# Attention scores in halves of 64 rows with 320 columns, masks as 64x64 triangles

## The chip, the cores and the metric

The kernel runs on one core of a Trainium2 chip. The metric is the device time of one execution in microseconds (us). The core has five engines that run beside each other and meet at semaphores: TensorE (PE, matmuls from SBUF into PSUM), VectorE (DVE), ScalarE (ACT), GpSimd (POOL) and SyncE (SP, which issues transfers). PSUM has 8 banks of 128 partitions with 512 f32 columns each.

## What is computed

A layer of attention and a mixture of experts on 4 x 1024 tokens of width 256, with 16 heads of width 16. What matters here is the attention, cut from the reference:

```python
xn = _layernorm(x, axis=-1)
q, k, v = heads(q), heads(k), heads(v)            # (4, 16, 1024, 16) each, from xn
attn = jnp.einsum('bhqd,bhkd->bhqk', q, k) / math.sqrt(DK)
mask = jnp.abs(idx[None, :] - idx[:, None]) > WINDOW      # WINDOW = 128
attn = jnp.where(mask[None, None], -1000000000.0, attn)
p = jax.nn.softmax(attn, axis=-1)
out = jnp.einsum('bhqk,bhkd->bhqd', p, v)
```

Each query sees the 128 keys on either side and itself. In tiles of 128 rows a tile of queries meets at most three tiles of keys: the previous one (a triangle of it), its own (whole), and the next one (a triangle).

## The kernel before

Projection, routing and experts come first (to about 740 us of the span), then the block `attend`, then `merge` (output projection, from about 1128 us). `attend` works through 64 pairs of batch and head in 16 groups of 4 heads (HG). A group has 8 rows j of 128 positions (TT). The scores are computed twice.

Query side, one group ahead: `scores_q` (matmul at L1459) has 128 queries on the partitions and up to 384 keys along the columns, in a ring of three banks (S1). DVE's `maxima` (L1626) adds the mask `mask_q` and takes each query's maximum, as a negative minimum, into `nmax`; each is an instruction on the tile and a short one that reads the accumulator. `split_maxima` splits them into a high and a low bf16 part, `turn_maxima` (PE, L1494) transposes them, `copy_maxima` (DVE, L1645) and four small transfers of SP put them as two more rows below the queries' parts, so that the second product subtracts the maximum by itself.

Key side, in the group itself: `scores_k` (L1467) has 128 keys on the partitions and up to 384 queries along the columns, in a ring of three banks (S2). `masks` (L1452) adds -1e30 outside of the window by a matmul of the identity with two stored 128x128 triangles, 256 columns in one instruction (interior rows) or 128 (rows 0 and 7, the edge rows). ACT's exponential (L1566) writes the tile `pT` to SBUF; `values` (L1480) multiplies it with the values, four heads in four column groups of 32 rows of one bank.

PE's order is written out: in row j, for each of four heads a key score with its mask and a query score of the group ahead; then the values of the row before; then in rows 0, 2, 3 and 5 a turn (of maxima at 0 and 5, of four output tiles, L1503, at 2 and 3), whose results go through the same ring of three S1 banks. DVE follows: the four maxima of a row, between them the additions of the gathered expert rows (L1664, L1680), the two normalisations (L1652, L1655), the splits and copies. A query score waits until DVE has freed the bank of three entries before (`s1_free`); a key score waits for the exponential of three heads before (`p_ready`). The first 32 query scores are taken among the last blocks of the experts (`score`, L1146, not touched). PE's loop over groups holds two of them, DVE's and ACT's one; first and last groups are written out. The last group has no query side.

Of the kernel before, what the change touches and what calls it, by code (L numbers as in the profile page):

```python
# [81 lines left out]
IOTA = 6 * P + 2 * MB  # L82
# [5 lines left out]
PARTS = (0, CUT), (CUT, TT)  # L88
PACK, PACK_BITS = 4, 6
# [19 lines left out]
def project(nc, ctx, x, w_qk, w_vr, w_exp, c_f32, keep):  # L109
# [158 lines left out]
    def vector(dve):  # L268
# [161 lines left out]
        nc.vector.tensor_copy(cb[:, :], consts[:, P:6 * P]).then_inc(consts_ready, 1)  # L430
# [170 lines left out]
def route(nc, ctx, keep, w_exp, left):  # L601
# [75 lines left out]
    def vector(dve):  # L677
# [57 lines left out]
        def table():  # L735
            for c in range(MB):
                chain.done(nc.vector.scalar_tensor_tensor(
                    junk[:, :], ends, consts[:, 6 * P + c:6 * P + c + 1], one, ALU.is_le, ALU.mult,
                    accum_out=cols[:, c:c + 1]))
                chain.wait()  # L740
# [194 lines left out]
def opening_tiles(nc, ctx):  # L935
# [3 lines left out]
    def sem(name):  # L939
# [3 lines left out]
        "mask_q": sb("mask_q", [P, 3 * P]), "masked": sb("masked", [P, 2, 3 * P]), "nmax": sb("nmax", [P, HG, TT]),  # L943
# [9 lines left out]
def experts(nc, ctx, keep, w_exp):  # L953
# [45 lines left out]
    ident_b, mask_prev, mask_next = (keep["cb"][:, k * P:(k + 1) * P] for k in (0, 3, 4))  # L999
# [31 lines left out]
    with nc.Block() as block:  # L1031
# [180 lines left out]
        def _(dve):  # L1212
# [61 lines left out]
            dve.wait_ge(o["mask_ready"], 3)  # L1274
# [7 lines left out]
def attend(nc, ctx, keep, onorm, w_proj):  # L1282
# [7 lines left out]
    ident_b, mask_prev, mask_next = (cb[:, k * P:(k + 1) * P] for k in (0, 3, 4))  # L1290
    both_masks = cb[:, 3 * P:5 * P]
# [7 lines left out]
    def sems(name, n):  # L1299
# [8 lines left out]
    mask_q, masked, nmax, nmax_b, nmaxT, nrow_in, s1_ready, s1_free, hi_done, nmax_ready, dve_tick, pe_tick = (  # L1308
        opening[name] for name in ("mask_q", "masked", "nmax", "nmax_b", "nmaxT", "nrow_in", "s1_ready", "s1_free",
# [9 lines left out]
    va_const, va_ready = sem("va_const"), sem("va_ready")  # L1319
# [64 lines left out]

    def key_back(j, hh):


        return {0: 2, 1: 2, 2: 5}.get(j * HG + hh, 3)
# [28 lines left out]
    with nc.Block() as block:  # L1417
# [25 lines left out]
        def _(pe):  # L1443

            def masks(bank, i, n):

                if i in (0, TT - 1):
                    out, mask = (bank[:, n - P:n], mask_next) if i == 0 else (bank[:, 0:P], mask_prev)
                else:
                    out = bank[:, 0:n].rearrange("p (t q) -> p t q", t=3)[:, 0:3:2, :]  # L1450
                    mask = both_masks.rearrange("p (t q) -> p t q", t=2)
                return nc.tensor.matmul(out, ident_b, mask, start=False, stop=True, skip_group_check=True)  # L1452

            def scores_q(g, q, i, hh):


                lo, hi = window(i)
                reach(pe, s1_free, ahead_entry(g, i, hh) - (RING - 1))
                nc.tensor.matmul(ring_bank(ahead_entry(like(g), i, hh))[:, 0:(hi - lo) * P], qk[0:KS, q, 0, hh, i * P:(i + 1) * P],  # L1459
# [484 lines left out]
```

## Time and profile before

| | |
|---|---|
| time, median of 3 runs | 1368.24 us (1366.77 to 1371.7) |
| span of the profiled execution, first to last instruction | 1166.2 us |
| time of the median outside of that span | 202.0 us |
| PE busy | 1085.4 us (93%), 8297 matmuls |
| PE weight loads busy | 799.0 us (69%) |
| DVE busy | 767.9 us (66%) |
| ACT busy | 756.1 us (65%) |
| POOL busy | 622.2 us (53%) |
| mean granted clock of TensorE | 0.984 |

Busy times are unions: two instructions beside each other count once. Matmuls are pipelined and their ends are modelled, so that the distance of two starts says more than a duration. The shares are over the whole span; the attention block is a third of it and has to be read by itself.

### The profile page before, as it was taken

To read this page: it belongs to the slowest core of one execution; us is meant where nothing else is said; L and a number is where in the kernel's file an instruction comes from. 1 tells how busy PE (TensorE), PEld (TensorE's weight loads), DVE (VectorE), ACT (ScalarE), POOL (GpSimd) and SP (SyncE) were. 2 spreads that over 40 slices of the span, in tenths; PEclk is the share of its full clock that TensorE was granted. 3 is DMA by queue.
4 is the path that set the end of the run, shared out by engine and by line. 5 is a ranking of instruction groups with operands and counts; after the bars stand their busy time and mean duration, and the time that the engine had idled before them with its cause. 6 is when DMAs were issued, how large, how long until landed. Compare 5 with 4: busy or idle time off the path is not lost. (4 is left out here: it accounts for less than half of the span.)

```text
span 1166.2 us, 33945 instructions
## 1 busy us (share of the span) xinstructions
PE 1085.4 (93%) x8297; PEld 799.0 (69%) x8298; DVE 767.9 (66%) x2491; ACT 756.1 (65%) x1914; POOL 622.2 (53%) x658
## 2 busy tenths in 40 slices
PE   6989799599999999999999999699999999999999
PEld 3545456399999999999999999355545545455457
DVE  7777779734444444444444457589999998999933
ACT  2555367567777777777777776366666666666653
POOL 0444200176666666666666655466666666666620
PEclk9999899899999999999999999799999999999999
DMA  6888811278888888878877764366665576656413
GB/s 223 216 213 213 240 42 32 94 222 261 247 251 244 252 253 240 250 240 250 253 229 205 206 198 149 101 154 159 154 171 142 142 169 161 152 143 159 122 60 122
DMA packets 143000, 213.84 MB, mean 183 GB/s; under 512 B 19425, under 2 KB 115682, under 8 KB 142946
## 3 DMA queue, kind: packets, MB, share of 16 engines
q0 software_dynamic: 27648, 86.02, 27.6%
q1 hardware_dynamic: 70946, 84.42, 25.9%
q10 hardware_dynamic: 44352, 42.74, 10.6%
q8 instruction: 26, 0.43, 0.2%
q14 instruction: 28, 0.23, 0.1%
HBM read 142.59 MB, written 70.26 MB: 183 GB/s over the span
## 5 line engine op out<-in xcount | busy, mean ns | idle before, releaser
L1076 POOL DMA_INDIRECT xb<-token_rows,idx_ring_x x320 | 303.1, 947 | 179.2 <-issue 140.5
L1104 PE MATMUL psum<-xTe,wb_and_xT_all_or_onorm 128*128 128x128 f32 x2560 | 339.2, 276 | 0.0
L1724 POOL DMA_INDIRECT yg<-expert_rows,idx_ring x256 | 254.2, 993 | 122.5 <-PE psum L1452 45.3
L1227 DVE TENSOR_SCALAR ys<-psum,xb 128x256 f32<-128x256 f32 x320 | 154.9, 484 | 244.7 <-PE psum L1113 243.3
L1104 PEld LDWEIGHTS psum<-xTe,wb_and_xT_all_or_onorm 128*128 128x128 f32 x2560 | 312.4, 192 | 0.1
L1566 ACT ACTIVATE pT<-psum 128x384 f32<-128x384 f32 (+1 forms) x512 | 215.5, 467 | 135.6 <-PE psum L1452 127.7
L1626 DVE CUSTOM_DVE_ANT_0 masked<-psum,mask_q 128x384 f32<-128x384 f32 (+1 forms) x480 | 230.9, 518 | 20.6 <-PE psum L1459 17.2
L1177 ACT COPY wb_and_xT_all_or_onorm<-wb_and_xT_all_or_onorm 128x512 f32 x320 | 197.7, 619 | 18.5 <-SPq L1038 4.8
L1113 PE MATMUL psum<-wb_and_xT_all_or_onorm,aT 128*128 x640 | 191.8, 381 | 0.4 <-issue 0.2
L1163 ACT COPY xTe<-psum 128x256 f32<-128x256 f32 x320 | 119.1, 372 | 102.4 <-PE psum L1094 93.0
L1459 PE MATMUL psum<-qk 96*128 96x384 bf16 (+1 forms) x480 | 154.0, 321 | 29.7 <-DVE nmax L1626 18.4
L1467 PE MATMUL psum<-qk 98*128 98x384 bf16 (+1 forms) x512 | 163.0, 320 | 4.0 <-POOL va L1729 2.0
L1452 PE MATMUL psum<-consts_bf 128*128 128x256 bf16 (+1 forms) x512 | 134.4, 263 | 0.0
L1094 PE MATMUL psum<-ident,xb 128*128 128x128 f32 x640 | 123.3, 275 | 7.3 <-DMA xb<-token_rows,idx_ring_x 7.3
L1094 PEld LDWEIGHTS psum<-ident,xb 128*128 128x128 f32 x640 | 90.0, 141 | 40.2 <-DMA xb<-token_rows,idx_ring_x 8.4
L1459 PEld LDWEIGHTS psum<-qk 96*128 96x128 bf16 x480 | 47.2, 98 | 89.8 <-DVE nmax L1626 46.4
L1480 PE MATMUL psum<-pT,va 128*32 128x256 f32 (+1 forms) x1792 | 103.7, 343 | 0.0
L1218 DVE TENSOR_TENSOR aT<-gate,psum 128x128 f32<-128x128 f32 x320 | 89.0, 278 | 16.6 <-ACT gate L1170 13.9
L1113 PEld LDWEIGHTS psum<-wb_and_xT_all_or_onorm,aT 128*128 128x128 f32 x640 | 98.0, 192 | 2.2 <-issue 1.5
L1170 ACT ACTIVATE gate<-psum 128x128 f32<-128x128 f32 x320 | 88.3, 276 | 15.2 <-issue 12.8
L1664 DVE TENSOR_TENSOR yg<-yg 128x512 f32<-128x512 f32 (+1 forms) x128 | 79.5, 622 | 8.4 <-DMA yg<-expert_rows,idx_ring 8.3
L256 POOL TENSOR_TENSOR wb_and_xT_all_or_onorm<-rest,wb_and_xT_all_or_onorm 128x512 bf16<-128x512 f32 x32 | 37.7, 1177 | 84.3 <-ACT wb_and_xT_all_or_onorm L227 84.3
(143 smaller groups left out, 1143.0 us busy)
## 6 DMA issues: line engine op xcount, KB each, us to landing
expert_rows<-ys ACTq DMA_DIRECT2D x160, 256.0 KB
wb_and_xT_all_or_onorm<-in_w_exp SPq DMA_DIRECT2D x64, 384.0 KB, 4.2
qk<-q_stacks SPq DMA_DIRECT2D x32, 384.0 KB
q_stacks<-wb_and_xT_all_or_onorm SPq DMA_DIRECT2D x32, 192.0 KB, 2.7
qk<-k_parts SPq DMA_DIRECT2D x32, 192.0 KB
k_parts<-wb_and_xT_all_or_onorm SPq DMA_DIRECT2D x28, 192.0 KB, 3.1
token_rows<-rows SPq DMA_DIRECT2D x8, 640.0 KB, 4.3
xb<-token_rows,idx_ring_x POOLq DMA_INDIRECT x320
```

What stands on the lines that cost most here:

```text
L1076: nc.gpsimd.indirect_dma_start(out=xb[:, r, :], out_offset=None, in_=rows_d, in_offset=bass.IndirectOffsetOnAxis(ap=idx_ring[:, q, r:r + 1 ...
L1094: last = nc.tensor.transpose(row_bank(i, r)[:, h * P:(h + 1) * P], xb[:, r % XR, h * P:(h + 1) * P], ident[:, :])
L1104: last = nc.tensor.matmul(banks[GU + r % NB][:, part * P:(part + 1) * P], wgu[:, r % NW, h, part * I:(part + 1) * I], xT[:, r % NX, h, :], ...
L1113: nc.tensor.matmul(banks[Y + r % 2][:, 0:D], aT[:, r % NB, :], wb[:, bass.ds(at + 4 * I, D)], start=True, stop=True).then_inc(y_ready, 1)
L1177: nc.scalar.copy(wgu[:, r % NW, :, :].rearrange("p h c -> p (h c)"), wb[:, bass.ds(place_of(words, r) * WCOLS, 4 * I)]).then_inc(wgu_ready, 1)
L1227: nc.vector.tensor_scalar(ys[:, r // 2 % YR, r % 2, :], banks[Y + r % 2][:, 0:D], xb[:, r % XR, bass.ds(e + W_COL, 1)], None, ALU.mult).th ...
L1452: return nc.tensor.matmul(out, ident_b, mask, start=False, stop=True, skip_group_check=True)
L1459: nc.tensor.matmul(ring_bank(ahead_entry(like(g), i, hh))[:, 0:(hi - lo) * P], qk[0:KS, q, 0, hh, i * P:(i + 1) * P], qk[0:KS, q, 1, hh, l ...
L1467: nc.tensor.matmul(key_bank(j, hh)[:, 0:(hi - lo) * P], qk[0:KM, q, 1, hh, j * P:(j + 1) * P], qk[0:KM, q, 0, hh, lo * P:hi * P], start=Tr ...
L1566: nc.scalar.activation(pT[:, (j % 2) * HG + hh, 0:(hi - lo) * P], key_bank(j, hh)[:, 0:(hi - lo) * P], ACT.Exp).then_inc(p_ready, 1)
L1626: nc.vector.tensor_tensor_reduce(masked[:, (i * HG + hh) % 2, 0:(hi - lo) * P], ring_bank(place)[:, 0:(hi - lo) * P], mask_q[:, side:side ...
L1724: nc.gpsimd.indirect_dma_start(out=yg[:, h, k, :], out_offset=None, in_=y_d, in_offset=bass.IndirectOffsetOnAxis(ap=idx_ring[:, h, k:k + 1 ...
```

## The change

The array's 128 output rows are used as two halves of 64 (z = 0, 1), one matmul each. Half z of a tile meets only 128 + 64 + 128 = 320 positions of the other side, which begin 64 further on for z = 1. On the query side (interior rows) both halves write columns 0 to 320 of the bank, so that DVE reads 320 columns with one mask `mask_h` for both halves (it depends on the row modulo 64 alone); edge rows keep 256 columns and `mask_q`. On the key side half z writes columns z*64 to z*64 + 320 of a bank whose column 0 now stands for position (j - 1)*128 in each row j, edge rows too; the mask of a half is two 64x64 triangles, 128 columns (64 in edge rows). The two corners of 64x64 per bank which no half writes are set to -1e30 once, by six memsets of DVE ahead of the first group, for which PE waits (`corners`). The exponential reads the same number of columns as before. The constants get 128 more columns (64 KB), their bf16 copy 128 more, and DVE fills `mask_h` with three operations before the experts begin. The query scores taken in the experts' stage, the values and the turns are as before.

```diff
+HP = P // 2
+HW = 2 * P + HP
...
-        nc.vector.tensor_copy(cb[:, :], consts[:, P:6 * P]).then_inc(consts_ready, 1)
+        nc.vector.tensor_copy(cb[:, :], consts[:, P:7 * P]).then_inc(consts_ready, 1)
...
+            mask_h = o["mask_h"]
+            nc.vector.tensor_copy(mask_h[:, 0:HP], mask_both[:, 0:HP]).then_inc(o["mask_ready"], 1)
+            nc.vector.memset(mask_h[:, HP:2 * P], 0.0).then_inc(o["mask_ready"], 1)
+            nc.vector.tensor_copy(mask_h[:, 2 * P:HW], mask_both[:, HP:P]).then_inc(o["mask_ready"], 1)
...
+    def keys_of(i, z):
+        lo, hi = window(i)
+        return (lo * P, hi * P) if hi - lo < 3 else (lo * P + z * HP, lo * P + z * HP + HW)
...
             def scores_q(g, q, i, hh):
-                lo, hi = window(i)
                 reach(pe, s1_free, ahead_entry(g, i, hh) - (RING - 1))
-                nc.tensor.matmul(ring_bank(ahead_entry(like(g), i, hh))[:, 0:(hi - lo) * P], qk[0:KS, q, 0, hh, i * P:(i + 1) * P],
-                                 qk[0:KS, q, 1, hh, lo * P:hi * P], start=True, stop=True).then_inc(s1_ready, 1)
+                bank = ring_bank(ahead_entry(like(g), i, hh))
+                for z in range(2):
+                    a, b = keys_of(i, z)
+                    last = nc.tensor.matmul(bank[z * HP:(z + 1) * HP, 0:b - a],
+                                            qk[0:KS, q, 0, hh, i * P + z * HP:i * P + (z + 1) * HP],
+                                            qk[0:KS, q, 1, hh, a:b], start=True, stop=True)
+                last.then_inc(s1_ready, 1)
...
             def scores_k(g, q, j, hh):
-                lo, hi = window(j)
                 reach(pe, p_ready, g * (HG * TT) + (j * HG + hh - key_back(j, hh) + 1))
-                nc.tensor.matmul(key_bank(j, hh)[:, 0:(hi - lo) * P], qk[0:KM, q, 1, hh, j * P:(j + 1) * P],
-                                 qk[0:KM, q, 0, hh, lo * P:hi * P], start=True, stop=False, skip_group_check=True)
-                masks(key_bank(j, hh), j, (hi - lo) * P).then_inc(s2_ready, 1)
+                bank, zero = key_bank(j, hh), (j - 1) * P
+                for z in range(2):
+                    a, b = max(zero + z * HP, 0), min(zero + z * HP + HW, T)
+                    nc.tensor.matmul(bank[z * HP:(z + 1) * HP, a - zero:b - zero],
+                                     qk[0:KM, q, 1, hh, j * P + z * HP:j * P + (z + 1) * HP],
+                                     qk[0:KM, q, 0, hh, a:b], start=True, stop=False, skip_group_check=True)
+                for z in range(2):
+                    last = mask(bank[z * HP:(z + 1) * HP, :], j, z)
+                last.then_inc(s2_ready, 1)
+
+            def mask(half, j, z):
+                before, after = half[:, z * HP:(z + 1) * HP], half[:, 2 * P + z * HP:2 * P + (z + 1) * HP]
+                if j == 0:
+                    out, rows = after, mask_both[:, HP:P]
+                elif j == TT - 1:
+                    out, rows = before, mask_both[:, 0:HP]
+                else:
+                    out = half[:, z * HP:z * HP + 4 * P - HP].rearrange("p (n c) -> p n c", c=HP)[:, 0:5:4, :]
+                    rows = mask_both.rearrange("p (n c) -> p n c", c=HP)
+                return nc.tensor.matmul(out, ident_b[:, z * HP:(z + 1) * HP], rows, start=False, stop=True,
+                                        skip_group_check=True)
...
+            pe.wait_ge(corners, 6)
             pe.wait_ge(va_const, 2)
...
-                nc.scalar.activation(pT[:, (j % 2) * HG + hh, 0:(hi - lo) * P], key_bank(j, hh)[:, 0:(hi - lo) * P],
-                                     ACT.Exp).then_inc(p_ready, 1)
+                zero = (j - 1) * P
+                nc.scalar.activation(pT[:, (j % 2) * HG + hh, 0:(hi - lo) * P],
+                                     key_bank(j, hh)[:, lo * P - zero:hi * P - zero], ACT.Exp).then_inc(p_ready, 1)
...
+                if hi - lo < 3:
+                    n, mask = 2 * P, mask_q[:, 0 if i > 0 else P:2 * P if i > 0 else 3 * P]
+                else:
+                    n, mask = HW, mask_h[:, :]
+                nc.vector.tensor_tensor_reduce(masked[:, (i * HG + hh) % 2, 0:n], ring_bank(place)[:, 0:n], mask,
+                                               -1.0, -NEG, ALU.add, ALU.min,
                                                accum_out=nmax[:, hh, i:i + 1]).then_inc(s1_free, 1)
...
+            for k in range(3):
+                nc.vector.memset(banks[S2 + k][0:HP, HW:3 * P], NEG).then_inc(corners, 1)
+                nc.vector.memset(banks[S2 + k][HP:P, 0:HP], NEG).then_inc(corners, 1)
             one_by_one(dve, group)
...
+    f[:, 6 * P:6 * P + HP] = np.where(r % HP > c[:, 0:HP], NEG, 0.0)
+    f[:, 6 * P + HP:7 * P] = np.where(c[:, 0:HP] > r % HP, NEG, 0.0)
```

## Rows read from the trace of the kernel before

**Rows 1.** Busy time by stage (columns: stretch, length, then each engine's busy us and instructions, PEclk, DMA share, GB/s).

```profile
740.40:752.60 12.20, 7.72 (x35) 3.45 (x35) 2.52 (x12) 5.92 (x16) 8.82 (x10) 0.64 0.39 109
752.60:773.50 20.90, 18.97 (x176) 10.04 (x176) 18.63 (x70) 11.48 (x32) 15.38 (x16) 0.85 0.55 143
773.50:1107.50 334.00, 309.64 (x3052) 168.52 (x3050) 307.13 (x1176) 218.17 (x617) 222.30 (x224) 1.00 0.62 153
1107.50:1128.00 20.50, 18.45 (x195) 9.03 (x195) 8.52 (x19) 13.95 (x39) 7.72 (x7) 1.00 0.18 53
```

**Rows 2.** Waits between 700 and 1140 us (who waited for whom: us in total, times, longest).

```profile
PEld psum L1459 <- DVE nmax L1626: 46.4, 117, 5.3
...
DVE masked L1626 <- PE psum L1459: 17.2, 33, 1.9
DVE rec L1652 <- PE psum L1503: 14.1, 17, 4.6
```

**Rows 3.** Groups of instructions by line and shape, whole span (busy us, mean ns, then idle before).

```profile
L1626 DVE CUSTOM_DVE_ANT_0 masked<-psum,mask_q 128x384 f32<-128x384 f32 x360 | 186.3, 552 | 10.0 <-PE psum L1459 7.8
...
L1480 PE MATMUL psum<-pT,va 128*32 128x256 f32 x1024 | 82.3, 393 | 0.0
...
L1626 DVE CUSTOM_DVE_ANT_0 masked<-psum,mask_q 128x256 f32<-128x256 f32 x120 | 44.6, 418 | 10.7 <-PE psum L1459 9.4 <-PE psum L1494 1.1
```

**Rows 4.** Timeline of DVE over one group, 895 to 919 us (start us, us, engine, line).

```profile
895.05 0.56 DVE L1626 CUSTOM_DVE_ANT_0 masked<-psum,mask_q 128x384 f32<-128x384 f32 x1 [0.39 <-PE psum L1459]
...
902.58 0.08 DVE L1626 DVE_READ_ACCUMULATOR2_ANT nmax<- 128x1 f32 x1
...
904.01 0.08 DVE L1626 DVE_READ_ACCUMULATOR2_ANT nmax<- 128x1 f32 x1
904.47 0.26 DVE L1652 RECIPROCAL rec<-psum 128x16 f32<-128x16 f32 x1 [0.37 <-PE psum L1503]
...
914.66 0.42 DVE L1626 CUSTOM_DVE_ANT_0 masked<-psum,mask_q 128x256 f32<-128x256 f32 x1
...
915.00 0.42 DVE L1626 CUSTOM_DVE_ANT_0 masked<-psum,mask_q 128x256 f32<-128x256 f32 x1
...
916.76 0.43 DVE L1626 CUSTOM_DVE_ANT_0 masked<-psum,mask_q 128x256 f32<-128x256 f32 x1 [0.56 <-PE psum L1459]
...
918.90 0.56 DVE L1626 CUSTOM_DVE_ANT_0 masked<-psum,mask_q 128x384 f32<-128x384 f32 x1 [0.39 <-PE psum L1459]
```

**Rows 5.** Timeline of PE: heads of an edge row, heads and values of interior rows.

```profile
892.25 0.27 PE L1467 MATMUL psum<-qk 98*128 98x256 bf16 x1
...
892.53 0.27 PE L1467 MATMUL psum<-qk 98*128 98x256 bf16 x1
...
905.43 0.33 PE L1459 MATMUL psum<-qk 96*128 96x384 bf16 x1
905.60 0.33 PE L1467 MATMUL psum<-qk 98*128 98x384 bf16 x1
905.76 0.27 PE L1452 MATMUL psum<-consts_bf 128*128 128x256 bf16 x1
905.87 0.33 PE L1459 MATMUL psum<-qk 96*128 96x384 bf16 x1
906.13 0.86 PE L1480 MATMUL psum<-pT,va 128*32 128x256 f32 x16
906.92 0.34 PE L1467 MATMUL psum<-qk 98*128 98x384 bf16 x1
```

**Rows 6.** Busy time in the first group while the clock is low.

```profile
754.00:758.00 4.00, 4.00 (x26) 1.76 (x24) 4.00 (x14) 1.56 (x4) 3.09 (x4) 0.50 0.35 99
```

**Rows 7.** Timeline of DVE in the first group.

```profile
741.36 0.42 DVE L1626 CUSTOM_DVE_ANT_0 masked<-psum,mask_q 128x256 f32<-128x256 f32 x1 [1.86 <-PE psum L1459]
...
759.37 0.56 DVE L1626 CUSTOM_DVE_ANT_0 masked<-psum,mask_q 128x384 f32<-128x384 f32 x1 [0.87 <-PE psum L1459]
```

**Rows 8.** DMA queues between 780 and 850 us (packets, MB, share of 16 engines).

```profile
q8 instruction: 5, 0.08, 0.6%
```

More of the change, by code:

```diff
@@ L81 @@
 MINE = float(1 << 20)
-IOTA = 6 * P + 2 * MB
+IOTA = 7 * P + 2 * MB
 VALUE = IOTA + NB_ROUTED
@@ L737, in table @@
                 chain.done(nc.vector.scalar_tensor_tensor(
-                    junk[:, :], ends, consts[:, 6 * P + c:6 * P + c + 1], one, ALU.is_le, ALU.mult,
+                    junk[:, :], ends, consts[:, 7 * P + c:7 * P + c + 1], one, ALU.is_le, ALU.mult,
                     accum_out=cols[:, c:c + 1]))
@@ L998, in experts @@
     nmax, nmax_b, nmaxT, s1_ready, s1_free = (o[name] for name in ("nmax", "nmax_b", "nmaxT", "s1_ready", "s1_free"))
-    ident_b, mask_prev, mask_next = (keep["cb"][:, k * P:(k + 1) * P] for k in (0, 3, 4))
+    ident_b, mask_prev, mask_next, mask_both = (keep["cb"][:, k * P:(k + 1) * P] for k in (0, 3, 4, 5))
     score_bank = banks[PX + 1]
@@ L1289, in attend @@
     ident, cb, v_sb, idx8, banks, res = (keep[name] for name in ("ident", "cb", "v_sb", "idx8", "banks", "res"))
-    ident_b, mask_prev, mask_next = (cb[:, k * P:(k + 1) * P] for k in (0, 3, 4))
-    both_masks = cb[:, 3 * P:5 * P]
+    ident_b, mask_both = cb[:, 0:P], cb[:, 5 * P:6 * P]
     def sb(name, shape, dt=F32):
@@ L1307, in attend @@
     opening = keep["opening"]
-    mask_q, masked, nmax, nmax_b, nmaxT, nrow_in, s1_ready, s1_free, hi_done, nmax_ready, dve_tick, pe_tick = (
-        opening[name] for name in ("mask_q", "masked", "nmax", "nmax_b", "nmaxT", "nrow_in", "s1_ready", "s1_free",
+    mask_q, mask_h, masked, nmax, nmax_b, nmaxT, nrow_in, s1_ready, s1_free, hi_done, nmax_ready, dve_tick, pe_tick = (
+        opening[name] for name in ("mask_q", "mask_h", "masked", "nmax", "nmax_b", "nmaxT", "nrow_in", "s1_ready", "s1_free",
                                    "hi_done", "nmax_ready", "dve_tick", "pe_tick"))
@@ new lines, in scores_k @@
+            def scores_k(g, q, j, hh):
+                reach(pe, p_ready, g * (HG * TT) + (j * HG + hh - key_back(j, hh) + 1))
+                bank, zero = key_bank(j, hh), (j - 1) * P
[7 more added lines that the diff above has]
+                last.then_inc(s2_ready, 1)
@@ L1623, in maxima @@
                 dve.sem_inc(dve_tick, 1)
-                side = 0 if i > 0 else P
-                nc.vector.tensor_tensor_reduce(masked[:, (i * HG + hh) % 2, 0:(hi - lo) * P],
-                                               ring_bank(place)[:, 0:(hi - lo) * P],
-                                               mask_q[:, side:side + (hi - lo) * P], -1.0, -NEG, ALU.add, ALU.min,
+                if hi - lo < 3:
[4 more added lines that the diff above has]
+                                               -1.0, -NEG, ALU.add, ALU.min,
                                                accum_out=nmax[:, hh, i:i + 1]).then_inc(s1_free, 1)
```

24 lines of the change are left out of this document (8 added, 16 removed).

## The prediction

> **What bounds the kernel now.** I read the busy time by stage first. The attention groups whose query scores are taken inside the attention block fill 740 to 1107 us; in the long stage of 334 us, which is 14 of the 16 groups, TensorE (PE) is busy 309.6 and VectorE (DVE) 307.1, both 92 to 93%, at a granted clock of 1.00 [rows 1]. Two engines look equal, so the waits must say which one sets the pace. PE's weight loads for the query scores (L1459) wait 46.4 us for DVE's maxima (L1626); DVE waits 17.2 us for those scores, and of the 14.1 us at the reciprocal (L1652) much belongs to the last group, where nothing is behind it [rows 2]. DVE is the bound and PE is the one held back. The timeline of DVE confirms it: a group takes 918.90 - 895.05 = 23.85 us, and in it DVE has gaps at three places only: 0.37 before the reciprocal, 0.56 at the loop's end, and 0.39 before the first 384-wide maximum of a group [rows 4]. The 0.56 is put down to PE, but one group earlier PE was at its second head at 892.25 [rows 5], which is 916.10 a period later: the first head's score had long been sent. I take this gap as DVE's own loop branch and leave it.
>
> How much PE has in hand is read from start to start, since ends are modelled. An interior head (key score, mask, query score) takes 905.87 - 905.43 = 0.44: scores of 384 columns 0.16 to 0.17, the mask of 256 columns 0.11; an edge head takes 892.53 - 892.25 = 0.28. From the row's last score to the values it is 0.26, so 0.09 beyond that score's own columns; the 16 value matmuls 906.92 - 906.13 = 0.79 [rows 5]. An interior row is 4 x 0.44 + 0.09 + 0.79 = 2.65. A group of six interior rows (15.9), two edge rows (4 heads of 0.28, 0.09 and 0.79 each: 4.0), less shorter values in one row (0.3) and plus four turns (1.2) is near 20.8 us of the 23.85. PE has 3 us free per group.
>
> **The change, part by part.**
>
> (a) *DVE's maxima, 24 of 32 per group, 384 to 320 columns.* From start to start three 384-wide ones take 904.01 - 902.58 = 1.43, so one 0.477, and a 256-wide one 915.00 - 914.66 = 0.34 to 0.35 [rows 4]; the mean durations, 552 and 418, differ by 0.134 [rows 3]. 320 lies in the middle, half of 0.13 below: 0.411, so 0.066 saved. 24 x 0.066 = 1.58 us per group. The form with 320 columns is in no row; its bounds are the two neighbours (0 and 3.2 us per group), and both ends agree with one straight line, so I take the middle.
>
> (b) *PE's scores and masks in two halves.* If the halves of a pair stream side by side, a head costs 320 + 128 + 320 columns. At the 0.165 per 384 and 0.11 per 256 of [rows 5] (a line of 0.43 per 1000 columns) that is 0.138 + 0.058 + 0.138, plus some 0.007 for each second start: 0.355 for 0.44. That halves do run together is shown by the values: 1024 matmuls of 32 output rows with a mean of 393 ns would take 402 us one behind another, and their busy time is 82.3 [rows 3]; 16 of them fit in 0.79 us [rows 5]. They too read different moving data from the same partitions and write different partitions of one bank. Groups of 64 rows in bf16 are in no row. Bounds for a head: 0.34 (no overhead) and 2 x (0.138 + 0.058 + 0.138) = 0.67 (no overlap). I take 0.355, nearest to the values. PE's work falls by 24 x 0.087 = 2.1 us per group, none of which the end sees directly, since DVE is the bound.
>
> (c) *Changes of the array's shape.* Today scores to values costs 0.09 beyond the columns, and values back to scores is part of the 0.79 [rows 5]. That stays. New: the four turns per group keep 128 columns, so after them there is another change of shape, 4 x 0.1 = 0.4 us of PE per group. The Trainium skill, "TensorEngine Tiling (Array Packing)", Key Properties, says that changing the tiling mode drains TensorE; the trace agrees (0.09 in rows 5).
>
> (d) *What is late next.* PE cannot run ahead of DVE by more than the ring of three banks, so per row there is a fixed chain: DVE releases a bank, PE puts the row's last query score there, then values, perhaps a turn, then the next key score, mask and query score. Where DVE's three remaining maxima and its other work take longer than this, nothing shows; where they don't, DVE waits. In row 3 it is late today: bank released at 902.66, reciprocal at 904.47, a chain of 1.81 of which DVE covers 1.44 [rows 4]. After the change the chain is about 1.80 (only the query score is shorter, by 0.02) and DVE covers 0.2 less, so the 0.37 becomes 0.56: +0.19. At the group's start (0.39 before 918.90) the maxima are 256 wide and unchanged; the chain loses 0.1 in key score, mask and query score and gains 0.1 by the shape change behind the turn: 0. In row 4 the chain without turn is 1.65 and DVE has 1.23 and some half us for the split of the maxima on it; the other rows carry additions of gathered rows or a normalise between the maxima, more than the split takes. No other wait opens.
>
> So a steady group: 23.85 - 1.58 + 0.19 = 22.46. 14 x 1.39 = 19.5 us.
>
> (e) *First group.* Until 752.6 DVE waits for the gathered rows; nothing is gained there. Then the clock is at half (0.50, which is 1.2 GHz, for 754 to 758, with PE busy 4.00 of 4.00 [rows 6]); in the stretch before it, where the clock averaged 0.64, PE was busy for 7.72 of 12.20 only [rows 1]. There PE sets the pace (0.87 wait at 759.37 [rows 7]): three heads save 0.17 each, eight more 0.087 each, 1.2; the twelve 384-wide maxima after that save 0.8. With a little for the second wait: 2.2 us.
>
> (f) *Last group*: no maxima; key scores, masks, exponentials and values follow each other over 20.5 us [rows 1]. A key score with its mask ends 0.08 earlier, about twice per row, less the shape changes: 0.8 us (bounds 0 and 1.5).
>
> (g) *Preparation.* 64 KB more of constants, 128 more columns in one cast, three small operations ahead of the experts, six memsets of 64x64 in the banks, for which PE now waits. DVE sits idle 1.86 us just before its first maximum [rows 7], which hides the memsets. I charge 0.3 us for the rest.
>
> Sum: 19.5 + 2.2 + 0.8 - 0.3 = 22.2 us. The profiled span 1166.2 becomes 1144. The profiled execution has no time of its own beyond its span; the median of 1368.24 lies 202 us above it, outside of the span, where no edit falls. 1368.2 - 22.2 = 1346.
>
> The exponentials keep their widths and read their corner from presets: nothing there changes.
>
> **Where the skill speaks against it.** "TensorEngine Tiling (Array Packing)" of the Trainium skill, Feature Incompatibilities, says that column tiling excludes the fast weight load. The skill's "TensorE: Matmul & The Clock Gate", LDWEIGHTS, gives about P/1.2 ns for P columns; as an estimate from that page a half of 64 columns takes 53 ns, and two, if one behind the other, 107 behind a mask of 58. By this estimate a head would be 0.05 longer. That leaves PE some 3.5 us free per group and lengthens the chains of (d) by 0.05 to 0.1; the sum would give 1348.
>
> **Rivals.**
>
> R1, the halves do not overlap (slower). A head costs 0.67. PE's group is then 20.8 + 24 x 0.23 + 8 x 0.2 (an edge head goes from 640 to 1088 columns) + 0.4 = 28.3, PE becomes the bound, 28.5 - 23.85 = 4.6 a group: +65, with the first and last groups +74: 1442. It decides once a head costs more than about 0.56, where PE's group passes 23.85. For it: no row with 64-row halves. Against: the values. 7%.
>
> R2, partial overlap: the halves run together, but starts, loads or semaphores add 0.1 to 0.2 per head. PE's chains then show at most rows; gain 4 to 15 us, 1353 to 1364. 12%.
>
> R3, PE's loop body no longer fits where instructions are kept. PE's loop body of two groups grows by 2 x 32 x 6 = 384 matmuls and weight loads. In the first groups 5 packets of the instruction queue took 0.6% of 16 engines' 70 us, 1.3 us each [rows 8]; within the steady loop none are fetched today. If one is waited for at each of 6 passes: +8 (1354); if six are: +47 (1393). 5%.
>
> R4, the clock. PE idles more (3 us free become 4.7 per group) and might be granted 0.50 in places, as in the first group. At twice the durations an interior head costs 0.71 and the values 1.6, a group about 36 us. A tenth of the stage so: 14 x 0.1 x 13.5 = 19 us more, 1365; all of it, 1535. Against: with the idle that PE has today the stage kept 1.00 [rows 1]. 3%.
>
> R5, DVE's waits vanish too because PE arrives earlier than I think: 0.37 + 0.39 more per group, +0.19 not lost: 13 us more, 1333. 6%.
>
> **How the numbers follow.** My forecast, 1346 (own range 1339 to 1353), has 67%. The range of 8 in 10 takes in most of R2 and part of R5: 1337 to 1362. A difference under 0.5% (6.8 us) I call no change: 1361.4 to 1375. Faster: forecast, R5, most of R2 and R3's mild end, 0.87; same 0.04; slower, R1 with the worse ends of R3 and R4, 0.09.
>
> **What would show it.** The 320-wide maximum start to start at 0.41; a group of 22.4 to 22.5; the wait of the reciprocal for L1503 at 0.5 to 0.6 per group; second halves starting under 0.01 us behind the first; an interior head without waits near 0.355; PE's wait for DVE up from 46 us. Wrong if halves start 0.13 apart, if the instruction queue moves packets between 850 and 1080, or if DVE waits for L1459's successor in rows other than the first.

## The result, and the profile after

The changed kernel takes 1393.62 us (median of 4 runs, 1389.3 to 1394.15), the kernel before 1368.69 beside it (1366.77 to 1371.7): ratio 1.0169, 95% interval 1.0147 to 1.0191, slower where the forecast was 1346. One plain fact is needed to read any number below: both kernels were met in two kinds of executions, in which the kernel before takes 1167 us or about 1370 to 1382, one kind throughout a series of runs, and both found on one and the same chip at different times. I call them short and long, and compare only within a kind. The trace before is a short one; the result compares long ones.

The changed kernel's trace (span 1387.3 us, execution 1389.3) is long too. Busy time by stage: the projection, the experts, fourteen attention groups, the last group, the merge (columns as in [rows 1]).

```profile
0.00:231.00 231.00, 191.37 (x777) 110.37 (x778) 180.39 (x478) 122.85 (x221) 56.07 (x63) 0.97 0.55 159
231.00:847.00 616.00, 551.85 (x3881) 477.66 (x3883) 243.57 (x715) 351.56 (x967) 312.76 (x341) 0.98 0.64 189
888.60:1325.00 436.40, 334.23 (x4399) 191.84 (x4402) 293.26 (x1176) 214.58 (x619) 234.02 (x224) 0.88 0.44 117
1325.00:1346.00 21.00, 17.80 (x225) 8.93 (x229) 7.06 (x15) 13.13 (x36) 6.57 (x6) 0.81 0.13 39
1346.00:1387.00 41.00, 37.23 (x224) 30.93 (x213) 14.95 (x36) 12.54 (x34) 0.00 (x0) 1.00 0.30 103
```

The experts' stage, in which no line of the diff runs, of the kernel before (its short trace):

```profile
231.00:740.00 509.00, 504.51 (x3873) 467.94 (x3873) 237.44 (x709) 371.44 (x958) 311.48 (x339) 0.99 0.76 229
```

The same 3870-odd matmuls fill 509 us of a short execution and 616 of a long one; PE is busy 99% of the short stretch and 90% of the long one. In the attention stage, 14 groups in 334 us with PE at 93% and DVE at 92% [rows 1] have become 14 in 436, both engines far from full (77 and 67%) at a mean clock of 0.88 instead of 1.00. So no engine is "the bound" in the sense of the prediction: each of them waits. The waits from 888 to 1325 us say on whom, over the attention stage as there (columns as in [rows 2]):

```profile
ACT pT L1594 <- PE psum L1494: 193.7, 129, 2.7
POOL yg L1757 <- PE psum L1494: 143.0, 88, 2.9
DVE masked L1657 <- PE psum L1463: 84.7, 88, 1.8
...
PEld psum L1463 <- DVE nmax L1657: 20.4, 44, 1.5
```

PE's wait for DVE fell from 46.4 to 20.4 and DVE's for PE rose from 17.2 to 84.7 [rows 2], partly because the two traces are of different kinds: the kernel before's own long trace (experiment 11) has 33.8 and 63.5. VectorE's single instructions last as forecast. By line and shape, same stretch, answering to [rows 3]:

```profile
L1657 DVE CUSTOM_DVE_ANT_0 masked<-psum,mask_h 128x320 f32<-128x320 f32 x336 | 153.0, 486 | 55.5 <-PE psum L1463 53.5 <-PE psum L1529 1.0 <-DVE nmaxT L1675 0.2
...
L1463 PE MATMUL psum<-qk 96*64 96x320 bf16 x672 | 113.3, 334 | 31.8 <-DVE wb_and_xT_all_or_onorm L1685 18.7 <-issue 6.8 <-DVE nmax L1657 3.4
...
L1657 DVE CUSTOM_DVE_ANT_0 masked<-psum,mask_q 128x256 f32<-128x256 f32 x113 | 45.6, 423 | 48.9 <-PE psum L1463 31.3 <-remote 16.3 <-issue 0.3
```

486 ns lies between the 552 and 418 of [rows 3]. TensorE's matmuls are a little longer in the mean than in a short trace (320 columns: 334 ns here, 309 in experiment 2), as the clock is at half for part of this stretch. DVE's timeline at an edge row (to [rows 4]) and PE's beside it (to [rows 5]):

```profile
1100.18 0.48 DVE L1657 CUSTOM_DVE_ANT_0 masked<-psum,mask_h 128x320 f32<-128x320 f32 x1
...
1100.60 0.49 DVE L1657 CUSTOM_DVE_ANT_0 masked<-psum,mask_h 128x320 f32<-128x320 f32 x1
...
1102.51 0.42 DVE L1657 CUSTOM_DVE_ANT_0 masked<-psum,mask_q 128x256 f32<-128x256 f32 x1 [1.08 <-PE psum L1463]
...
1103.97 0.42 DVE L1657 CUSTOM_DVE_ANT_0 masked<-psum,mask_q 128x256 f32<-128x256 f32 x1 [1.03 <-PE psum L1463]
```

```profile
1101.14 0.30 PE L1463 MATMUL psum<-qk 96*64 96x256 bf16 x2
1102.72 0.30 PE L1476 MATMUL psum<-qk 98*64 98x256 bf16 x2 [1.28 <-ACT pT L1594]
1102.84 0.22 PE L1494 MATMUL psum<-consts_bf 128*64 128x64 bf16 x2
1103.00 0.30 PE L1463 MATMUL psum<-qk 96*64 96x256 bf16 x2
```

The 320-wide maxima follow each other at 0.42, where 0.411 was worked out. But the query score sent at 1101.14 (0.30 long) is taken by DVE only at 1102.51, 1.37 us after its start; and PE stands still for 1.28 in a row with nothing heavy in it. This is the rule in long traces: where DVE has to wait for a query score, its maximum starts 0.5 to 0.6 us after the score in the short traces (medians of the twelve middle groups, 0.57 and 0.52 for the two kernels of experiments 1 and 2) and 1.8 and 2.2 us after it in the long ones (experiments 11 and 12). The instruction queue moved 8 packets between 900 and 1300 us (to [rows 8]):

```profile
q8 instruction: 8, 0.13, 0.1%
```

The kernel before moved 6 in the same stretch of its long trace, so code loading is not what sets the two apart.

### The profile page after: what moved, and what is told of

It reads as the page before. It is cut to its first block and busy times, and to the rows that moved or that the text cites. A ratio compares the mean times of both kernels' runs of the same rounds, so it can differ in the third digit from the quotient of the medians.

```text
span 1387.3 us, 36963 instructions
## 1 busy us (share of the span) xinstructions
PE 1158.4 (84%) x9801; PEld 833.7 (60%) x9802; DVE 759.3 (55%) x2500; ACT 730.4 (53%) x1914; POOL 634.9 (46%) x658
## 5 line engine op out<-in xcount | busy, mean ns | idle before, releaser
L1757 POOL DMA_INDIRECT yg<-expert_rows,idx_ring x256 | 266.5, 1041 | 221.7 <-PE psum L1494 150.3
L1106 PE MATMUL psum<-xTe,wb_and_xT_all_or_onorm 128*128 128x128 f32 x2560 | 350.7, 280 | 8.9 <-issue 6.0
L1476 PE MATMUL psum<-qk 98*64 98x320 bf16 (+2 forms) x1024 | 177.4, 338 | 73.1 <-ACT pT L1594 46.0
L1115 PE MATMUL psum<-wb_and_xT_all_or_onorm,aT 128*128 x640 | 200.3, 395 | 35.1 <-DVE ys L1229 23.8
L1463 PE MATMUL psum<-qk 96*64 96x320 bf16 (+1 forms) x960 | 167.5, 340 | 48.0 <-DVE wb_and_xT_all_or_onorm L1685 18.7
L1657 DVE CUSTOM_DVE_ANT_0 masked<-psum,mask_h 128x320 f32<-128x320 f32 x360 | 164.1, 486 | 67.0 <-PE psum L1463 57.6
L1476 PEld LDWEIGHTS psum<-qk 98*64 98x64 bf16 x1024 | 66.0, 119 | 129.4 <-ACT pT L1594 71.0
L1494 PE MATMUL psum<-consts_bf 128*64 128x128 bf16 (+1 forms) x1024 | 129.2, 234 | 0.0
L1463 PEld LDWEIGHTS psum<-qk 96*64 96x64 bf16 x960 | 64.5, 123 | 95.6 <-DVE wb_and_xT_all_or_onorm L1685 25.2
L1506 PE MATMUL psum<-pT,va 128*32 128x256 f32 (+1 forms) x1792 | 115.2, 372 | 0.0
```

Of the source, the lines that this page charges most:

```text
L1106: last = nc.tensor.matmul(banks[GU + r % NB][:, part * P:(part + 1) * P], wgu[:, r % NW, h, part * I:(part + 1) * I], xT[:, r % NX, h, :], ...
L1115: nc.tensor.matmul(banks[Y + r % 2][:, 0:D], aT[:, r % NB, :], wb[:, bass.ds(at + 4 * I, D)], start=True, stop=True).then_inc(y_ready, 1)
L1463: last = nc.tensor.matmul(bank[z * HP:(z + 1) * HP, 0:b - a], qk[0:KS, q, 0, hh, i * P + z * HP:i * P + (z + 1) * HP], qk[0:KS, q, 1, hh, ...
L1476: nc.tensor.matmul(bank[z * HP:(z + 1) * HP, a - zero:b - zero], qk[0:KM, q, 1, hh, j * P + z * HP:j * P + (z + 1) * HP], qk[0:KM, q, 0, h ...
L1494: return nc.tensor.matmul(out, ident_b[:, z * HP:(z + 1) * HP], rows, start=False, stop=True, skip_group_check=True)
L1657: nc.vector.tensor_tensor_reduce(masked[:, (i * HG + hh) % 2, 0:n], ring_bank(place)[:, 0:n], mask, -1.0, -NEG, ALU.add, ALU.min, accum_ou ...
```

## The experiments

Each runs beside the kernel before on the same chip. "Group" is the period of the 32 exponentials of a group, the mean of the twelve groups in the middle of the trace. The code cuts are shortened. The letters (theory A, B, C and so on) are those of the expectations, each written before its run.

**1 and 2. Both kernels again, unedited.**

> The kernel before, unchanged. In the changed kernel's profile the experts' stage, whose code the change leaves alone, takes 605 us (237 to 842) against 500 in the profile of before, and the span is 1387 of a time of 1389, while the span of before was 1166 of a time of 1368. Theory A (the profiled execution of before was of another kind than its timed ones): the span is near 1366 now, the experts' stage near 605 and a group of attention near 29.5 us in place of 23.85. Theory B (the change itself slows the experts' stage, by the place of its buffers or its constants): the span is near 1166, the experts' stage 500, a group 23.85, and 200 us lie outside of the span.

> The changed kernel, unchanged. 1390 to 1394 us, ratio 1.017 to before. Under theory A its experts' stage is as long as that of before (605) and its attention is the longer by some 20 us (about 31 us a group against 29.5); under B the experts' stage alone makes the difference of the two spans.

This series was a short one, which neither expectation had as its main case: the kernel before 1167.99, ratio 1.0006 (0.9997 to 1.0016); the changed kernel 1149.01, ratio **0.9836** (0.982 to 0.9853), 18.3 us less. Both theories of experiment 1 fell in part: the span is 1166 as theory B had it, but its own span and its time agree within 2 us, so there are no 200 us outside of a span. Groups 23.87 and 22.63. The changed kernel's waits from 772 to 1085 us and its timelines of DVE and PE:

```profile
PEld psum L1463 <- DVE nmax L1657: 27.3, 79, 0.7
...
DVE masked L1657 <- PE psum L1463: 15.9, 42, 1.0
...
DVE rec L1682 <- PE psum L1529: 7.8, 14, 0.6
```

```profile
887.05 0.49 DVE L1657 CUSTOM_DVE_ANT_0 masked<-psum,mask_h 128x320 f32<-128x320 f32 x1 [0.31 <-PE psum L1463]
...
894.81 0.49 DVE L1657 CUSTOM_DVE_ANT_0 masked<-psum,mask_h 128x320 f32<-128x320 f32 x1
...
895.86 0.26 DVE L1682 RECIPROCAL rec<-psum 128x16 f32<-128x16 f32 x1 [0.56 <-PE psum L1529]
...
899.26 0.49 DVE L1657 CUSTOM_DVE_ANT_0 masked<-psum,mask_h 128x320 f32<-128x320 f32 x1 [0.49 <-PE psum L1463]
...
906.10 0.42 DVE L1657 CUSTOM_DVE_ANT_0 masked<-psum,mask_q 128x256 f32<-128x256 f32 x1 [0.71 <-PE psum L1463]
```

```profile
895.97 0.30 PE L1463 MATMUL psum<-qk 96*64 96x320 bf16 x2
896.11 0.30 PE L1476 MATMUL psum<-qk 98*64 98x320 bf16 x2
896.25 0.22 PE L1494 MATMUL psum<-consts_bf 128*64 128x128 bf16 x2
896.31 0.30 PE L1463 MATMUL psum<-qk 96*64 96x320 bf16 x2
```

An interior head takes 0.34, and the trace's own start times put a second half 3 to 5 ns behind the first. The wait before the reciprocal is the forecast 0.56. The group shown is one of the longer ones; seven of the twelve middle groups take 22.42 to 22.46 us on DVE.

**3 and 4. Halves on one side only.** Changed kernel with `scores_k` and its masks (3) or `scores_q` and its 384-wide maxima (4) as before:

```
-  for z in range(2): matmul(bank[z*HP:(z+1)*HP, ...], qk[..., half z], qk[..., a:b])
+  matmul(bank[:, 0:(hi - lo) * P], qk[..., j * P:(j + 1) * P], qk[..., lo * P:hi * P])
```

> Only the query scores in halves, with DVE's maxima of 320 columns; key scores and masks as before in full width. Theory C (DVE's shorter maxima gain, the doubled count of matmuls and weight loads on PE costs): 64 more PE instructions per group than before instead of 192, so between: with the gain of 1.58 us per group kept, faster than before, 1350 to 1360. Theory D (the clock falls to half once per group because PE, with halves, is busy for less of the time): one third of the columns saved on PE, so about as the change or a little better, 1375 to 1390.

> Only the key scores and masks in halves; query scores and the maxima of 384 columns as before. Theory C: 128 more PE instructions per group, no gain at DVE: slower than the changed kernel or like it, 1390 to 1405. Theory D: two thirds of PE's saving and no saving at DVE, so PE is idle for more of a group: clock at half once per group, 1390 to 1400.

Short: 1214.86, ratio 1.0383 (1.0308 to 1.0458), and 1191.21, ratio 1.0202 (1.0185 to 1.0219); groups 26.33 and 24.98. All four theories missed. (Of the four runs of (3) two take 1206 and two 1223; the trace is of one at 1223, whose first two groups take 44.1 and 33.2 us; the others are all at 26.33.) The stretch from 800 to 1100 us of each:

```profile
800.00:1100.00 300.00, 300.00 (x2843) 126.32 (x2836) 243.74 (x949) 185.61 (x493) 175.00 (x181) 0.99 0.55 138
```

```profile
800.00:1100.00 300.00, 300.00 (x3400) 136.04 (x3392) 270.61 (x1009) 195.34 (x529) 198.18 (x193) 1.00 0.59 148
```

PE is busy without a gap: now it is the bound. Such a head changes the array's shape twice. Against the 20.8 us of work of the prediction, less the columns that the edit saves (24 x 0.027 = 0.6 and 24 x 0.079 = 1.9), a group is 6.1 us longer in both, over 64 changes: an estimate of **0.095 each**, close to the 0.09 of [rows 5]. In this kernel halves pay only where everything between two values is in halves.

**5 and 6. TensorE's part alone, VectorE's part alone.** (5) the changed kernel with 384-wide maxima; (6) the kernel before with maxima over 320 columns, the last 64 left out:

```
(5) - n, mask = HW, mask_h[:, :]
    + n, mask = 3 * P, mask_h[:, :]        # columns 320 to 383: NEG
(6) + n = min((hi - lo) * P, 2 * P + P // 2)
    - tensor_tensor_reduce(masked[..., 0:(hi - lo) * P], ...)
    + tensor_tensor_reduce(masked[..., 0:n], ...)
```

> The changed kernel, but the 24 maxima per group read 384 columns again (the last 64 of the mask are the lowest value, so they never win). TensorE's halves alone, VectorE's part undone. Theory V (VectorE is the bound, the halves only give TensorE room): a group stays near 23.9 us, the time is within 4 us of the kernel before, about 1165 where that has 1167. Rival T (TensorE is held up somewhere, and its shorter heads are themselves part of the gain): a group of 23.0 to 23.4, 1155 to 1160. Rival X (the halves and the extra shape changes cost TensorE more than they save): over 24.3 a group, 1172 or more.

> The kernel before, but its 384-wide maxima read only their first 320 columns (the last 64 columns of those scores are left out of the maximum). VectorE's part alone, TensorE unchanged at 0.44 per interior head and 20.8 us of work per group. Theory V: VectorE still sets the pace, a group of 22.3 to 22.7, 1144 to 1150, as good as the whole change (1149). Rival T: TensorE with its full scores comes late in more rows, a group of 23.0 to 23.5 and 1154 to 1162; then the halves are what lets VectorE's saving through.

Short: 1165.01, ratio 0.9973 (0.9962 to 0.9983), group 23.77; and 1153.62, ratio 0.9872 (0.9855 to 0.9888), group 22.91. 3.5 and 14.9 us add up to 18.4 of the 18.3. Theory V (VectorE is the bound) holds for (5) and for four fifths of the gain; (6) misses V's range by 4 us, toward T (TensorE is late in places): TensorE's shorter scores let another 0.28 us a group through.

**7 to 10. More instructions on an engine that has nothing to compute.** In SyncE's group, kernel before (7, 9) and changed (8, 10), N = 100 (7, 8) or 330 (9, 10):

```
   maxima(q, 1, turn_entry(g, M_LATE))
+  for _ in range(N): sp.sem_inc(spare, 1)
```

> The kernel before, with 100 increments of a semaphore that nobody waits for added per group on SyncE, 1600 in all: more events per microsecond (about 4 more beside the 36 recorded instructions per us of the attention stage), no work on any engine that computes. Theory N (the late completions seen in the first comparison come from the number of instructions and events per us): completions of TensorE come later, the time rises by 5 to 60 us. Rival P (they come from something of that execution's own, not from this kernel's number of events): no change, 1166 to 1169.

> The changed kernel with the same 100 increments per group. It issues 46 recorded instructions per us in the attention stage where the kernel before issues 36. Theory N: it is nearer to the limit, so it loses more than the kernel before does with them, 10 to 100 us, and falls behind it (over 1170). Rival P: no change, 1146 to 1150, ratio to the kernel before 0.982 to 0.985.

Short: 1168.63, ratio 0.9998 (0.9988 to 1.0007), and 1147.87, ratio 0.9833 (0.9812 to 0.9854). No effect, as rival P expected.

> The kernel before with 330 increments of an unused semaphore per group on SyncE (100 of them took 57 to 58 ns each and left the time at 1168.6). 330 x 0.058 = 19 us of a group's 23.9 on SyncE, so the rate of events is up by 17 per us, to 53 recorded instructions per us, nearly all the time; SyncE keeps some 4.5 us of a group for its DMA issues. Theory N (the number of instructions and events per us limits): completions late and engines idle in bursts, the group at 25 us or more, over 1185. Rival P (that number is no limit at this height): 1167 to 1170. Side effect in both: if SyncE's own issues (indices, query rows) come too late, single groups are longer by up to 2 us, seen as waits for a DMA, up to 1185.

> The changed kernel with the same 330 increments per group: 64 recorded instructions per us, twice what it reached in the first comparison (31 to 34). Theory N: the limit is passed, a group of over 26 us, slower than the kernel before by 3% or more. Rival P: 1147 to 1151, and 19 us of increments per 22.5 us group leave SyncE 3.5 us; if that is too little for its issues, waits for DMAs and up to 1170.

This series was a long one (the kernel before 1381.23): 1636.19, ratio 1.1855 (1.1808 to 1.1901), and 1637.22, ratio 1.186 (1.1827 to 1.1894), groups 46.8 and 47.3. Theory N's ranges, over 1185 and slower by 3% or more, are met, but this is no clean count of instructions, as SyncE itself became late. Waits of (9) from 900 to 1500 us:

```profile
PE psum L1470 <- DMA qk<-nmaxT: 210.1, 13, 18.6
```

But it shows the disturbance by itself. An increment follows the last by 57 to 59 ns. In (7), of the 1584 distances within groups none lies between 0.5 and 1 us; in (13), the same kernel in a long series, 167 do; in (9), of 5264, 285 do, 0.69 us each, 197 us together. So even an engine that reads no data and waits for nobody is held up in a long execution. It is no common standstill: in (9) a matmul starts in 81% of these stalls, but in only 34% of equally long stretches of increments without a stall; for ScalarE it is the other way round, 15 and 37%. SyncE is held up mostly while TensorE starts work.

**11 and 12. Both kernels again.**

> The kernel before once more. Where this execution takes about 1370 to 1381: Theory N (a limit on instructions and their events per us) expects the experts' stage at 600 to 610 us instead of 497, the projection as long as ever (231), a group of 29 to 30 us at some 29 recorded instructions per us, single instructions as long as ever. Rival C (a slower clock or slower engines) expects longer single instructions everywhere, the projection too. Where it takes 1167, it repeats the first repeat.

> The changed kernel beside the kernel before. Theory N: where the kernel before takes 1370 to 1381, this one takes 1.4 to 2.2% more (some 1390 to 1405), since it issues 192 instructions more per group; where that takes 1167, this one takes 1149. Rival M (the first comparison was an accident of its own): 1.5% faster whatever the kernel before takes.

A long series: 1374.02 beside 1370.19, and 1395.86, ratio **1.0201** (1.015 to 1.0253). The result is no accident of one series: rival M is out, theory N's 1.4 to 2.2% is met. Now the kernel before has a long trace:

```profile
0.00:231.00 231.00, 190.89 (x779) 109.97 (x780) 180.17 (x475) 123.05 (x222) 56.67 (x63) 0.97 0.55 160
231.00:847.00 616.00, 552.51 (x3871) 478.51 (x3871) 242.30 (x707) 350.05 (x956) 310.86 (x337) 0.98 0.64 189
891.00:1310.00 419.00, 337.31 (x3066) 172.02 (x3066) 311.70 (x1179) 214.17 (x622) 236.48 (x226) 0.96 0.49 122
```

The projection and the experts are as in the changed kernel's; the 14 groups take 419 for 436. One line of the experts from 300 to 700 us, first of the short trace of experiment 1, then of this one:

```profile
L1227 DVE TENSOR_SCALAR ys<-psum,xb 128x256 f32<-128x256 f32 x258 | 124.9, 484 | 210.2 <-PE psum L1113 209.6 <-issue 0.2
```

```profile
L1227 DVE TENSOR_SCALAR ys<-psum,xb 128x256 f32<-128x256 f32 x216 | 104.2, 483 | 210.4 <-PE psum L1113 193.9 <-issue 10.8 <-remote 3.2
```

484 and 483 ns each: VectorE is no slower (rival C is out), 258 are done in one case and 216 in the other. All engines together start 35.4 instructions per us in the experts of short executions and 29.7 in long ones (300 to 700 us); in attention 36.4 and 29.0 (kernel before), 46.8 and 33.8 (changed). The projection, at 12, is not stretched. No single rate is the limit: 29.0 and 33.8 are both long executions.

**13 and 14.** The kernels of experiments 7 and 6 in the same long series.

> The kernel before with 100 unused increments per group on SyncE, which cost nothing where that kernel takes 1167. Where it takes 1370 to 1381, Theory N: 1600 instructions more at 14 to 40 ns each (the change's own 3008 cost some 43 us there against its gain elsewhere, 14 ns each; 330 increments cost 48 ns each), 22 to 64 us, 1400 to 1445. Rival P (only TensorE's own instructions count): within 4 us of the kernel before.

> The kernel before with maxima that read only 320 of 384 columns (the last 64 columns left out of the maximum): less work for VectorE, not one instruction more or less. Where the kernel before takes 1167 it gave 1153.6, ratio 0.987. Where that takes 1370 to 1381, Theory N: VectorE's work is not what limits there, so little is left of it, 0 to 6 us, ratio 0.996 to 1.000. Rival M: 0.987 again.

(13) 1378.22, ratio 1.0062 (1.0026 to 1.0098): 8 us for 1600 increments, 5 ns each (2 to 8), well under N's 14 and over the 4 us that P allowed, so both missed. (14) 1375.62, ratio 1.0049 (1.002 to 1.0077): the shorter maxima, worth 14.9 us in a short execution, are worth nothing here; they cost 0.2 to 0.8%, which N (0.996 to 1.000) did not expect either.

**15 and 16. Instructions without columns, columns without instructions.** Kernel before; (15) every score in two matmuls of half the columns; (16) scores of 320 columns and masks of 128, with the maxima of (6). (15) starts a bank twice before the mask is added, so its key scores are not those of the kernel before; (16) leaves out 64 columns and one of two masks:

```
(15) - matmul(bank[:, 0:384], stationary, moving[0:384])
     + matmul(bank[:, 0:192], stationary, moving[0:192])
     + matmul(bank[:, 192:384], stationary, moving[192:384])
(16) - scores 384, both_masks 2 x 128        + scores 320, mask_prev 128
```

> The kernel before, each score matmul of 384 (or 256) columns as two of 192 (or 128) with the same weights: 1984 more instructions on TensorE (992 matmuls, 992 weight loads; the change has 3008 more), not a column more or less, no other shape of the array. Where the kernel before takes 1370 to 1381 - Theory K (the number of TensorE's instructions costs): two thirds of the change's loss, 1380 to 1400. Theory L (a TensorE with fewer columns idles, its clock falls to half more often, and that costs): no change, 1366 to 1374. Where it takes 1167, both: TensorE has 3 us per group free and needs at most 1.5 to 3 of them for loads that no longer hide, 1167 to 1185.

> The kernel before with 320 columns in the scores, 128 in the masks and 320 in the maxima of interior rows (the last 64 columns of those scores and one of their two masks are left out): TensorE's columns as few as in the changed kernel, VectorE's work the same as there, but not one instruction more and no halves. Where the kernel before takes 1370 to 1381 - Theory L: as slow as the changed kernel, 1385 to 1400, the clock at half for 120 us or more of the attention stage. Theory K: 1360 to 1375, as with VectorE's part alone. Where it takes 1167: VectorE sets the pace, 1144 to 1150 as the changed kernel (1149), or less than that where its shape changes cost.

Long (the kernel before 1381.89): (15) 1398.19, ratio 1.0117 (1.0099 to 1.0134); (16) 1391.66, ratio 1.0064 (1.0042 to 1.0086). With its 1984 instructions (15) costs 16.3 us, 8.2 ns each (6.9 to 9.3), the two thirds of the change's loss that theory K said; L's "no change" is out. (16) in microseconds lies over K's range and within L's, 1385 to 1400, but the kernel before took 1381.89 in this series, 12 us more than beside the result: by the ratio it loses 0.64%, a third of the change's 2.0, where L had it lose as much as the change. Of the 0.64%, 0.49 come with the short maxima already (14, another series), and the missing columns add 0.15, within the intervals. Neither edit was run in a short series, so that (15)'s loss belongs to long executions alone is not shown.

**17 and 18. TensorE's halves with maxima as before, beside the whole change.**

> The changed kernel with maxima of 384 columns, as before (TensorE's halves alone, 3008 more of its instructions). Where the kernel before takes 1370 to 1382: Theory K (TensorE's instructions are the cost): 1984 of them cost 1.2%, so 3008 cost 1.8%, 1392 to 1402, as slow as the whole change. Theory L (less work, more idling and a lower clock; VectorE's shorter maxima alone gave +0.5%, narrow scores on top +0.15%): 0.2 to 0.6% slower, 1372 to 1388. Where the kernel before takes 1167, 1165 as in the run of it before.

> The changed kernel in the same job, to be set against the kernel without the short maxima. Theory K: both the same within 0.3%, at 1.7 to 2.1% over the kernel before. Theory L: this one 1% or more above the other. Where the kernel before takes 1167, 1149.

Long (1371.49): 1397.6, ratio 1.0196 (1.0167 to 1.0225), and 1398.73, ratio 1.0212 (1.0184 to 1.0239). K: the halves alone cost all of it, 26.1 us with 3008 more instructions, **8.7 ns each** (7.6 to 10.3), and the short maxima give nothing back. The same kernel was 3.5 us faster than the kernel before in a short series (5).

## Why the prediction was wrong, step by step

**The step that failed** is in the sum: "the median of 1368.24 lies 202 us above it, outside of the span, where no edit falls". The result's own execution has 2 us outside of its span. In the timed executions these 202 us lie inside the span: by the traces of experiments 1 and 11, 109 between 231 us and the first exponential (741.9 and 850.5), 98 from there to the last (382 and 480), 0 behind it (41.6 both), 207 in all for these two. The trace that I read was of an execution whose bound was not that of the timed ones: in those, VectorE's shorter maxima are worth nothing (14), so the 1.58 us per group of term (a), 22 us in 14 groups and nearly the whole sum, was not there to be had, and the halves, which were to cost nothing, cost 26.1 us (17). The table that stands ahead of the prediction, with a span 15% below the median, was the warning; 14 groups of 23.87 could not be assumed for it.

**Bound DVE, PE held back**: right in short executions (5 and 6: DVE's part is 14.9 of 18.3 us), wrong in the timed ones (14: it is worth nothing).

**(a) 0.411 per maximum**: right in both (0.41; 0.42 at 1100.18).

**(b) 0.355 per head, halves side by side**: right, 0.34 at 895.97, second half 3 to 5 ns behind. R1 (no overlap) and R2 are out; R1's own sum gives 28.3 us a group and goes on with 28.5, 3 us too much in the end. The Trainium skill's "TensorEngine Tiling (Array Packing)", Feature Incompatibilities, denies such halves the fast weight load; by an estimate from that rule I had put a head 0.05 longer, and the trace shows none of it.

**(c) 0.1 per change of shape**: right, 0.095 by 3 and 4. The same page's Key Properties say that changing the mode drains TensorE; the runs agree that a change costs time, by that number; by what it comes they do not show.

**(d) waits**: the reciprocal's 0.56 is as forecast, in each of the middle groups, and the wait ahead of a group's first 320-wide maximum went from 0.39 to 0.31 (887.05). "No other wait opens" was wrong: at the start of row 5, where the trace before has 0.11 that I did not count, DVE waits 0.18 in most groups and 0.49 in one (899.26), and in single groups 0.71 at a row without a wait elsewhere (906.10). So most groups take the forecast 22.46 or a little less, two take 23.2 to 23.3, and the mean is 22.63: 14 x 1.24 = 17.4 instead of 19.5. The sign "PE's wait for DVE up from 46 us" did not come, even in short executions: from 742 to 1110 us it fell from 45.6 to 36.1.

**(e) to (g)**: first group 30.55 to 29.02, 1.5 for 2.2. The span fell by 18.7 (1165.6 to 1146.9), which leaves -0.2 for the last group and the preparation, for +0.5. DVE still sits idle ahead of its first maximum, as in [rows 7], 0.96 us in the result's trace, so that preparation is covered:

```profile
847.41 0.42 DVE L1657 CUSTOM_DVE_ANT_0 masked<-psum,mask_q 128x256 f32<-128x256 f32 x1 [0.96 <-PE psum L1463]
```

By size the whole working gave 22.2 us, and short executions show 18.3: even for its own kind of execution the forecast was 4 us too good.

**R3** (instruction fetch): out. Its sign did come, 2 packets between 850 and 1080 us in the changed kernel's short trace, which gains all the same; in the long traces it is 8 packets in 400 us beside 6 for the kernel before. **R4** (the clock): it came. From 700 us on the clock was at half for 138.6 us in the result's execution and for 77.1 in the kernel before's long trace (21.2 and 17.1 in the short ones). Half is 1.2 GHz. PE stands still in gaps of over 0.3 us for 5.4 us of a group (kernel before, 29.84) and 6.9 (changed, 31.41) in the long traces, and for 0.9 and 1.3 in the short ones, whose twelve middle groups have no low clock at all. But the profiled execution of (13) had only 34.4 us of it and took 1364.42, where the kernel before's fastest took 1363.84, and (16) had 114.7 with no instruction more and lost 0.6%: the low clock goes with the loss, and no run separates what part of the 2% it carries. An estimate, from the mean clock of all executions: (14) and (16), without one instruction more, are at half for 30 and 59 us more than the kernel before beside them and lose 5.4 and 9.8 us, 0.17 to 0.18 per us. The change (12) is at half for 85 us more, (17) for 84, (15) for 22. At that price the clock would carry 14 to 15 of the change's 26 us and 4 of (15)'s 16, and an instruction more would cost 4 to 6 ns instead of 8 to 9. The low clock may as well follow from the loss. **R5**: no, VectorE's waits grew.

**What the runs show in the failed step's place.** In long executions dense stages are stretched, with VectorE's single instructions as long as ever; completions are taken later (1.8 to 2.2 us for 0.5 to 0.6); there a kernel with more TensorE instructions is slower by 8.2 to 8.7 ns for each, though they add no column (15, 17), the cost of the low clock included; and what the change saves VectorE is worth nothing (14, 17 against 18). The 2% is shown to come with TensorE's halves (17). That it is their 3008 instructions rather than the idling and low clock that go with them is argued from (15) and (16), not shown.

**Open**: what the disturbance is. In the long traces a third of the records of semaphore updates is missing (15,427 kept for 23,615 in the same kernel's short trace); whether what loses them also holds the engines up, no run shows. Every execution compared here was recorded with its span and clock, so an obvious rival stands untested: that the recording itself is what holds up a long execution, and more so a kernel with more instructions. Whether an instruction of another engine costs less than one of TensorE is not settled either (2 to 8 ns against 6.9 to 10.3). Nor is it known what makes an execution long.

## What to carry to other kernels

Before pricing an edit, set the span of the trace against the timed median: here every execution whose time and span are both known has them within 2.2 us of each other, and the one trace that was 202 us short was of another kind of execution, with another bound. Splitting matmuls to save columns is a trade of columns for instructions: here it gained 18 us where VectorE was the limit and lost 25 in the stretched executions. Where tiles of another shape are used, keep all work between two changes in one shape: a change costs about 0.095 us here, and two per head were enough to make TensorE the bound.

## What was not expected of the hardware

Both kinds of execution on the same chip, 1167 and 1370 to 1382 us for one kernel, with nothing in between in any series. Stalls of 0.69 us on SyncE between increments that wait for nothing, more often while TensorE is starting matmuls. Halves of 64 rows start 3 to 5 ns apart and their weight loads of 64 columns, 108 to 110 ns each in the records, cost the head nothing. Shorter maxima on VectorE made a long execution no faster but 0.2 to 0.8% slower.
